# Third graph layer of a graph and expert network: the gathered table in three bf16 parts instead of fp32 rows

## The reference, cut to what matters

```
x = x + gnn0(layernorm(x))        # two segment sums over all edges: h + sum(h[src]) -> MLP 256-512-512, then 512-512-256
x = x + attention(layernorm(x))   # 64 slices per head, 8 heads
x = x + gnn1(layernorm(x)):       # the layer that is changed
      h = x @ W; dinv = rsqrt(deg)
      out = segment_sum(h[src] * (dinv[src] * dinv[dst]), dst) + b
      relu(batchnorm(out))
x = x + experts(layernorm(x))     # 8 experts, 2 chosen per node, 256-512-256
```

## Time and profile before

| | us |
|---|---|
| time before, median of 3 runs | 4495.84 (4486.59 to 4501.65) |
| the profiled execution | 4527.99 |
| its span | 4526.2 |
| busy in the span: PE / PEld / DVE / ACT / POOL | 3407.3 / 2256.3 / 1481.5 / 497.8 / 2794.2 |

### The profile page before, as it was taken

How to read it: one execution, slowest core, us unless ns; L and a number is a source line. 1 busy time by engine, 2 the same in 40 slices (tenths; PEclk the granted TensorE clock), 3 DMA queues, 4 the chain that set the end, 5 groups by cost and what they waited for, 6 DMA issues and landing times. The chain is left out here.

```text
span 4526.2 us, 40559 instructions
## 1 busy us (share of the span) xinstructions
PE 3407.3 (75%) x12357; PEld 2256.3 (50%) x12359; DVE 1481.5 (33%) x5707; ACT 497.8 (11%) x1161; POOL 2794.2 (62%) x2815
## 2 busy tenths in 40 slices
PE   3577777878878889899999976566556656658997
PEld 2354444545453444444444455345444444438986
DVE  5112121212121433444333445234343343442221
ACT  4010000000110000000000002000000000003432
POOL 4666666666646666666666502666666666635664
PEclk7788888988889999999999987777777778769998
DMA  6333333433349666666666527334334333327887
GB/s 199 90 112 112 111 110 110 131 111 111 109 128 330 194 198 200 193 190 194 195 201 205 170 104 240 108 114 123 115 117 128 115 114 114 119 80 174 203 210 188
DMA packets 321341, 687.10 MB, mean 152 GB/s; under 512 B 58976, under 2 KB 148300, under 8 KB 320854
## 3 DMA queue, kind: packets, MB, share of 16 engines
q0 software_dynamic: 169712, 474.01, 37.9%
q10 hardware_dynamic: 86448, 110.35, 7.4%
q1 hardware_dynamic: 64970, 100.14, 6.8%
HBM read 592.43 MB, written 99.13 MB: 153 GB/s over the span
## 5 line engine op out<-in xcount | busy, mean ns | idle before, releaser
L280 POOL DMA_INDIRECT s_edge_rows<-table,w_src_idx x2538 | 2495.4, 983 | 1235.3 <-issue 712.6
L320 PE MATMUL s_psA<-s_edge_rows,s_onehot 128*128 128x257 f32 (+2 forms) x4932 | 1695.0, 487 | 212.1 <-DMA s_edge_rows<-table,w_src_idx 92.3
L320 PEld LDWEIGHTS s_psA<-s_edge_rows,s_onehot 128*128 128x128 f32 x4932 | 1012.6, 210 | 758.6 <-issue 635.1
L295 DVE TENSOR_SCALAR s_onehot<-w_iota_row,w_dst_l 128x128 f32<-128x128 bf16 x2466 | 531.6, 296 | 28.5 <-PEq L149 16.4
L2031 POOL DMA_INDIRECT acc_rows<-s_y,s_tnode x105 | 166.3, 1584 | 130.7 <-DVE s_y L2154 98.8
L1011 PE MATMUL s_psM<-s_h1T,s_w1b 128*128 128x512 f32 (+2 forms) x448 | 195.2, 582 | 52.5 <-ACT s_h1T L913 49.0
L330 PE MATMUL s_psA<-s_edge_rows,s_early 128*128 128x257 f32 (+2 forms) x648 | 221.3, 468 | 10.2 <-issue 9.0
L1017 PE MATMUL s_psM<-s_w2a,s_hT 128*128 128x512 f32 x392 | 196.3, 647 | 22.7 <-issue 16.6
L2179 PE MATMUL s_psU<-s_xT,s_w 128*128 128x128 f32 x1680 | 208.2, 278 | 0.2 <-ACT s_xT L2085 0.2
L2179 PEld LDWEIGHTS s_psU<-s_xT,s_w 128*128 128x128 f32 x1680 | 199.3, 195 | 0.6 <-issue 0.6
L2189 PE MATMUL s_psD<-moe_w,s_hT 128*128 x840 | 199.5, 381 | 0.0
(11 more groups left out here) (364 smaller groups left out, 2802.6 us busy)
## 6 DMA issues: line engine op xcount, KB each, us to landing
s_w<-in_L_ffn_W_dram SPq DMA_DIRECT2D x105, 512.0 KB
s_edge_rows<-table,w_src_idx POOLq DMA_INDIRECT x2538
s_swT<-swt_rows SPq DMA_DIRECT2D x12, 1024.0 KB
table<-s_trow ACTq DMA_DIRECT2D x11, 1024.0 KB
own_rows<-s_own ACTq DMA_DIRECT2D x11, 1024.0 KB
s_self_h<-own_rows ACTq DMA_DIRECT2D x11, 1024.0 KB
swt_rows<-s_swT ACTq DMA_DIRECT2D x11, 1024.0 KB
extra_rows<-w_zeros SPq DMA_DIRECT2D x7, 896.0 KB
```

Of the source, the lines that this page charges most:

```text
L280: pool.indirect_dma_start(self.rows[:, g % self.SLOTS, t, :], None, self.table, bass.IndirectOffsetOnAxis(ap=src_idx[:, at:at + 1], axis=0 ...
L295: last = nc.vector.tensor_scalar(into[:, t, :], iota_row[:, q * P:(q + 1) * P], dst_l[:, at + t:at + t + 1], None, ALU.is_equal)
L320: last = nc.tensor.matmul(banks[b % 2][:, 0:w], self.onehot[:, g % self.AHEAD, t, :], self.rows[:, g % self.SLOTS, t, col:col + w], start= ...
```

## The change

The third table becomes `[NPAD, 3 * D]` in bf16: a row holds the high part bf16(v), the middle part bf16(v - high), and the low part bf16(v - high - middle), 1536 bytes instead of 1024. A new table `v3_rows` holds v in fp32 for each node's own row.

- In s3 ACT copies vrow into the high part (128x1024 fp32 to bf16), DVE subtracts it into the single buffer `rest`, ACT copies `rest` into the middle part, DVE subtracts that into the low part, and ACT stores the three parts (768 KB for a superblock). There are three sets of parts. DVE does the low part of superblock sb-5 and the rest of superblock sb-4 at the end of the loop's turn sb, and the remaining five after the loop. The store of fp32 rows now goes to `v3_rows`.
- In s4 the rows and one-hots are bf16. PE makes two matmuls for each tile from the same one-hot: 512 columns (high and middle) and 256 columns (low), both starting at column 0 of the bank. So the bank holds high sums plus low sums in columns 0 to 255 and middle sums in columns 256 to 511, and DVE's `close` adds both halves in two dependent additions (new semaphore `s_half`). The spare path does the same.
- `begin` loads the own rows from `v3_rows`.

The diff:

```diff
--- before.py
+++ after.py
@@ -131,7 +131,8 @@
         swt_rows = dram("swt_rows", [NB, P, KH * P], FP32)
         x2_rows = dram("x2_rows", [NPAD, D], FP32)
         extra_rows = dram("extra_rows", [NPAD, D], FP32)
-        table3 = dram("table3", [NPAD, D], FP32)
+        table3 = dram("table3", [NPAD, 3 * D], BF16)
+        v3_rows = dram("v3_rows", [NPAD, D], FP32)
 
         acc_rows = dram("acc_rows", [NPAD + P, D], FP32)
         xl3_rows = dram("xl3_rows", [NPAD + P, RG], FP32)
@@ -1311,7 +1312,7 @@
 
         with ExitStack() as stack:
             S = Scope(stack, "s3")
-            LOADS, ROWSETS, BATCH = 6, 4, ((0, 4), (4, 8), (8, 11), (11, SB + 1))
+            LOADS, ROWSETS, PARTSETS, BATCH = 6, 4, 3, ((0, 4), (4, 8), (8, 11), (11, SB + 1))
             tokT = S.sb("tokT", [P, KD, HID])
             rnorm = S.sb("rnorm", [P, KH])
             stok = S.sb("stok", [P, KH, P])
@@ -1336,6 +1337,8 @@
             rstd = S.sb("rstd", [P, NB])
             shift = S.sb("shift", [P, NB])
             vrow = S.sb("vrow", [P, ROWSETS, 4, D])
+            parts = S.sb("parts", [P, PARTSETS, 4, 3 * D], BF16)
+            rest = S.sb("rest", [P, 4, D])
             psM = [S.ps(f"psM{i}") for i in range(4)]
             psX = [S.ps(f"psX{i}") for i in range(3)]
 
@@ -1369,7 +1372,12 @@
             s_scale = S.sem("row_scales")
             s_v = S.sem("scaled_rows")
             s_x2s = S.sem("x2_stored")
-            s_sto = [S.sem(f"table_stored{i}") for i in range(ROWSETS)]
+            s_sto = [S.sem(f"rows_stored{i}") for i in range(ROWSETS)]
+            s_table = [S.sem(f"table_stored{i}") for i in range(PARTSETS)]
+            s_high = S.sem("high_parts")
+            s_rest = S.sem("rests")
+            s_mid = S.sem("middle_parts")
+            s_low = S.sem("low_parts")
             block = stack.enter_context(nc.Block())
 
             def size_of(sb):
@@ -1452,6 +1460,20 @@
                         last = v.bn_aggr(mv[:, q, :], stat[:, q, :])
                     return last
 
+                def part(sb, i):
+                    return parts[:, sb % PARTSETS, 0:size_of(sb), i * D:(i + 1) * D]
+
+                def rest_of(sb):
+                    nb = size_of(sb)
+                    dve.wait_ge(s_high, sb + 1)
+                    if sb:
+                        dve.wait_ge(s_low, sb)
+                    v.tensor_tensor(rest[:, 0:nb, :], vrow[:, sb % ROWSETS, 0:nb, :], part(sb, 0), ALU.subtract).then_inc(s_rest, 1)
+
+                def low(sb):
+                    dve.wait_ge(s_mid, sb + 1)
+                    v.tensor_tensor(part(sb, 2), rest[:, 0:size_of(sb), :], part(sb, 1), ALU.subtract).then_inc(s_low, 1)
+
                 for sb in range(SB + 1):
                     for h in range(2):
                         q, n = sb * 4 + 2 * h, min(2, size_of(sb) - 2 * h)
@@ -1465,6 +1487,14 @@
                         if sb + 1 == end:
                             ch.link(last)
                             scales(i)
+                    if sb >= 5:
+                        low(sb - 5)
+                    if sb >= 4:
+                        rest_of(sb - 4)
+                for sb in range(SB - 4, SB + 1):
+                    low(sb)
+                    if sb < SB:
+                        rest_of(sb + 1)
 
             @block.scalar
             def _(act):
@@ -1491,6 +1521,15 @@
                 for c in range(2, 4):
                     ac.activation(mix[:, c, :], psX[0][:, (c - 2) * D:(c - 1) * D], ACT.Copy, scale=ssum[:, c:c + 1]).then_inc(s_mix, 1)
 
+                def middle(sb):
+                    nb = size_of(sb)
+                    act.wait_ge(s_rest, sb + 1)
+                    ac.activation(parts[:, sb % PARTSETS, 0:nb, D:2 * D], rest[:, 0:nb, :], ACT.Copy).then_inc(s_mid, 1)
+
+                def store(sb):
+                    act.wait_ge(s_low, sb + 1)
+                    act.dma_start(block_rows(table3, sb * 4, size_of(sb)), parts[:, sb % PARTSETS, 0:size_of(sb), :]).then_inc(s_table[sb % PARTSETS], 16)
+
                 for i, (start, end) in enumerate(BATCH):
                     act.wait_ge(s_scale, i + 1)
                     for sb in range(start, end):
@@ -1502,8 +1541,20 @@
                             last = ac.activation(vrow[:, at, j, :], x1[:, b, :], ACT.Identity, bias=shift[:, b:b + 1], scale=rstd[:, b:b + 1])
                         last.then_inc(s_v, 1)
                         act.wait_ge(s_v, sb + 1)
-                        act.dma_start(block_rows(table3, sb * 4, nb), vrow[:, at, 0:nb, :]).then_inc(s_sto[at], 16)
+                        act.dma_start(block_rows(v3_rows, sb * 4, nb), vrow[:, at, 0:nb, :]).then_inc(s_sto[at], 16)
                         act.dma_start(block_rows(x2_rows, sb * 4, nb), x1[:, blocks_of(sb), :]).then_inc(s_x2s, 16)
+                        if sb >= PARTSETS:
+                            act.wait_ge(s_table[sb % PARTSETS], sb // PARTSETS * 16)
+                        ac.activation(parts[:, sb % PARTSETS, 0:nb, 0:D], vrow[:, at, 0:nb, :], ACT.Copy).then_inc(s_high, 1)
+                        if sb >= 1:
+                            middle(sb - 1)
+                        if sb >= 2:
+                            store(sb - 2)
+                middle(SB)
+                store(SB - 1)
+                store(SB)
+                for i in range(PARTSETS):
+                    act.wait_ge(s_table[i], 16 * len(range(i, SB + 1, PARTSETS)))
                 for i in range(ROWSETS):
                     act.wait_ge(s_sto[i], 16 * len(range(i, SB + 1, ROWSETS)))
                 act.wait_ge(s_x2s, 16 * (SB + 1))
@@ -1592,7 +1643,7 @@
 
             PRODUCT, NORM, TURNED, GATES = (0, 1, 2, 3), 4, (7, 8, 9, 10), 11
             CHOICE, RANK, PLACED, USED = 12, 16, (17, 18, 19, 20), (18, 19, 20, 21)
-            edges = Edges(S, table3, D, ((0, D),), FP32, 1, slots=6)
+            edges = Edges(S, table3, 3 * D, ((0, 2 * D), (2 * D, D)), BF16, 1, slots=6)
             w = S.sb("w", [P, KD, D])
             bias = S.sb("bias", [P, D])
             bmean = S.sb("bmean", [P, D])
@@ -1655,7 +1706,9 @@
             s_self = S.sem("self_rows")
             s_both_self = S.sem("self_rows_summed")
             s_x = S.sem("x2_rows")
+            s_half = S.sem("high_sums_copied")
             s_evac = S.sem("sums_copied")
+            s_spare = S.sem("high_spare_sums_added")
             s_tr = S.sem("sums_transposed")
             s_aggT = S.sem("transposes_copied")
             s_o = S.sem("graph_products")
@@ -1711,7 +1764,7 @@
                 def begin(s):
                     b0, nb = SUPER[s]
                     act.wait_ge(s_evac, b0 + 2)
-                    act.dma_start(self_v[:, 0:nb, :], block_rows(table3, b0, nb)).then_inc(s_self, 16)
+                    act.dma_start(self_v[:, 0:nb, :], block_rows(v3_rows, b0, nb)).then_inc(s_self, 16)
                     if s == 0:
                         act.wait_ge(edges.s_odone, 1)
                     act.dma_start(extra[:, 0:nb, :], block_rows(extra_rows, b0, nb)).then_inc(s_self, 16)
@@ -1784,7 +1837,9 @@
                 dve.sem_inc(s_w, 1)
 
                 def add_spare(k, at):
-                    v.tensor_tensor(edges.own[:, :], edges.own[:, :], psO[1][:, 0:D], ALU.add).then_inc(edges.s_oread, 1)
+                    v.tensor_tensor(edges.own[:, :], edges.own[:, :], psO[1][:, 0:D], ALU.add).then_inc(s_spare, 1)
+                    dve.wait_ge(s_spare, k + 1)
+                    v.tensor_tensor(edges.own[:, :], edges.own[:, :], psO[1][:, D:2 * D], ALU.add).then_inc(edges.s_oread, 1)
 
                 def group(b, g):
                     if b + 1 < NB and g < groups_of(b + 1):
@@ -1801,7 +1856,9 @@
                         v.tensor_tensor(self_v[:, 0:SUPER[s][1], :], self_v[:, 0:SUPER[s][1], :], extra[:, 0:SUPER[s][1], :], ALU.add).then_inc(s_both_self, 1)
                     dve.wait_ge(edges.s_used, groups_before(b + 1))
                     dve.wait_ge(s_both_self, s + 1)
-                    v.tensor_tensor(agg[:, q, :], self_v[:, q, :], psA[b % 2][:, 0:D], ALU.add).then_inc(s_evac, 1)
+                    v.tensor_tensor(agg[:, q, :], self_v[:, q, :], psA[b % 2][:, 0:D], ALU.add).then_inc(s_half, 1)
+                    dve.wait_ge(s_half, b + 1)
+                    v.tensor_tensor(agg[:, q, :], agg[:, q, :], psA[b % 2][:, D:2 * D], ALU.add).then_inc(s_evac, 1)
 
                 def largest(nb, i):
```

## The result

The changed kernel takes 4516.78 us (median of 6 runs, 4514.69 to 4518.34) against 4495.60 for the kernel before: ratio 1.0046, 95% interval 1.0035 to 1.0057. It is slower by 21 us; 4516 was predicted.

A forecast was written before the change was run, and what follows sets the result against it. It took s4 to be paced by POOL's 1.26 us per gather plus a stop per ring, and s3 by PE; 22 (s3) - 10 (PE) + 10 (wider rows) - 2 (tail) = +20 on 4495.84 gave 4516 us, range 4450 to 4545.

The forecast's parts named there:

- s3, +22: In s3, making and storing the three parts lengthens the stage's tail before s4's first gather by 22 us.
- a cycle of 5.7 us on ACT: In s3's tail, ACT's norms, copies and three issues take 5.7 us per superblock, where it had 3.1.
- Rival C: In s3, stores of parts saturate DMA; at 5 us a landing s3 costs +36, the whole 4540; chance 0.14.
- +10: In s4's gathers, rows of 1536 bytes instead of 1024 cost 10 us (ends 0 and +34).
- -10: In s4, a faster PE removes 10 us of the gathers' stops (ends 0 and -75).
- The tail: After s4's last gather, PE's remaining groups get a third shorter, worth -2 us.
- the lower end of the range: PE in s4: 768 bf16 columns at a column a cycle, 0.32 us a tile, saving a third, 190 us at most.
- 100 or more that were named as a sign: Sign of being right: PE's busy time in s4 falls by 100 us or more without the stage's length following.
- D: In s4, two weight loads per tile and the 1.2 GHz clock keep PE from getting faster: +32, 4528; chance 0.09.
- E: In s4, bf16 compares on DVE hold POOL's issue through the shared port: +90, 4606; chance 0.03.
- The stops: In s4's gathers, POOL stops some 3 us about once for each ring of 18 tiles: 47 stops.
- The floor of 141 us: In s4, 47 stops x 3.0 us remain whatever PE does, leaving 9 of the 150 us of idle.

The follow-up runs named there:

- e6: Changed kernel with five sets of parts in s3 instead of three and four places in the ring of attention loads instead of six: 4513.20 us, ratio 1.0037.
- e11: Changed kernel with s3's high parts copied by POOL instead of ACT: 4099.23 us against 4083.78 for the kernel before, ratio 1.0036.
- e7: Kernel before with eight slots (24 tiles) instead of six in s4's ring: 4501.54 us, ratio 1.0008.
- e1: Changed kernel with s3 as changed, but s4 gathering fp32 rows with fp32 one-hots as before: 4510.18 us, ratio 1.0047.
- e3: Changed kernel with s4 summing only the high part, a third of PE's work per tile, gathering the same 1536 bytes: 4505.03 us, ratio 1.0024.
- e4: Changed kernel with each pair of products made twice in s4, doubling PE's work per tile: 4535.07 us, ratio 1.0092.
- e12: Changed kernel itself, run once more beside the kernel before: 4512.78 us against 4490.94, ratio 1.0048.
- e5: Changed kernel with a table of two parts, rows of 1024 bytes, the middle part multiplied in place of the low: 4515.05 us, ratio 1.0037.

## Why the prediction was right

**s3, +22.** Right in size, and near in the times of its steps. Counted from the first product, the scales of the last batch were to end at 97.3 us and ended at 97.0; the last norm was to start at 112.8 and started at 111.2; the last store was to be issued at 120.3 and its two issues ran until 119.1; the stage was to be 21.5 longer and is 20.6. (The 21.5 is taken from an end of the stage before at 2781.4, where the prediction's own sum of rows gives 2782.03; from there it is 20.9.) ACT began s4 3.9 us after the end of the last issue, where 3.1 were counted, which made up for a part of the early steps. DVE's operations took 1.22 us as their neighbour in the earlier trace rows, ACT's 1.05 against 1.1. The text that summed it up, a cycle of 5.7 us on ACT, was right as a number (5.8) but not as the cause: the cycle holds waits, and taking work or waits off ACT (e6, e11) gave 1.5 us or nothing. Rival C's sign did appear, the landings being 5.4 us in the median, but its price was wrong: +36 for s3 at 5 us, where s3 is +20.6 and five sets of parts give back 1.5. (There is one more store in a superblock, three for two, not three more.)

**s4, 0.** Here the sum was right by luck: two terms, +10 and -10, were both too large and cancelled. Wider rows cost nothing (forecast +10), and PE's shorter work gave at most 3 or 4 us of gathers (forecast -10). In single executions these took 1210.2 (e7) and 1216.0 us (e1) with fp32 in s4, and 1210.7 to 1213.4 in five with the change's s4 as it is, which is hardly a difference. The interpolation between 973 and 1013 ns assumed that bytes make the difference; the mean stays at 974 with 1536 bytes. What makes sum 2's long gathers was not tried. The tail was to give 2, and nothing shows of it: from the last gather to POOL's first operation of the experts it is 50.9 us before and 52.5 after, and 51.3 to 61.0 in e1 and e7 with fp32, though PE's groups there got shorter. What bounds it was not looked for.

**PE.** It saves 22% per tile, not a third: the lower end of the range was optimistic, and the reason given for it misread the row, since a record of 0.243 us for 256 columns is 2.3 cycles a column at 2.4 GHz, not "nearly two". The Trainium skill ("FP8 and Floating Point Precision", "TensorE Precision Notes") counts four passes for an fp32 product, an estimate of a quarter less by its count (768 against 1024 columns), and the trace comes near it: 22% at 2.4 GHz (1.14 against 1.46 us for three tiles) and 23% at 1.2. Busy time fell by 71 us, not by the 100 or more that were named as a sign. An estimate says why: 22% of the 493 + 63 us of products would be 122, but all of PE's work ran at a granted clock of 0.71 instead of 0.76. D's half about the clock was right, its half about the weights wrong: the weight loads of the stage were busy 366 us instead of 557. The Trainium skill ("TensorE: Matmul & The Clock Gate", "What's actually happening") says that idle stretches lower the clock; e3 and e4 agree, 0.59 with PE busy 37% of s4 and 0.85 with 74%. None of it touched the end, where the forecast gave it 12 us.

**The premise that held the rest.** PE's speed does not set the pace of s4: a third of its work or twice, -4 and +15 us. With no stops the gathers take 1068.8 us (e11), POOL's pitch of 1.26 us alone, as the prediction had worked out (1066). E did not occur: DVE's bf16 compares took 274 instead of 298 ns, and the gathers beside them 974.

**The stops** (one each ring of 18 tiles) were wrong as a mechanism: with 24 tiles their time stays (130 us in e7 against 137 in e1), and in one set of runs they are absent with 18. The floor of 141 us that bounded PE's worth rested on them, so the small term for PE came out right for a wrong reason.

## What to carry to other kernels

Before making an engine faster, see what its neighbours' idle time does where the same loop runs with other loads: three sums with PE busy 737 to 1135 us lost about the same time, and the runs with a third and twice of PE's work confirmed what that said. Preparing a new format in a serial stage can cost far more than the engines' shares suggest: s3 is 20.6 us longer for 29 us more work on DVE (50.8 to 79.6 us busy) and 24 more on ACT (25.5 to 49.5), though they had been idle for half and three quarters of the stage, because the work of the last superblocks lies behind the last scales and nothing runs beside it. And compare stages, not spans: the untouched sums show which execution was the odd one.

## What the runs showed of the hardware

The kernel before took 4491 to 4497 us in all sets of runs but one and 4084 in that, in which the gathers ran almost without stops. Between the traces of e12 and e11, whose gathers are the same, the idle time of the gathers in s4 beyond 0.30 us each is 138 against 4 us (130 to 154 in all runs with stops), and the two graph sums are 245 us shorter together; the three streams of gathers make 390 of the 408 us between the two spans. The ratios to the kernel before stayed alike, 1.0036 for e11 and 1.0048 for e12, but 9% of the time of a kernel of 2538 gathers hung on something outside its program. What stops POOL for 2 to 5 us at the wait for a slot that PE has long used up stays open. It is hardly PE's work (e3, e4), not 18 against 24 tiles (e7), not the bytes of a gather between 1024 and 1536 (e5); and where it occurs, PE and DVE wait long for each other too (PE 185.7 us for DVE's close in the changed kernel, 14.4 in e11).
